# Passes 2 and 3 of a graph kernel: the type sums of all six dense blocks on VectorE

## The reference

```python
x = layernorm(x + wx * segment_sum(w**2 * wx[src], dst))            # layer 0
x = layernorm(x + out @ W2 + b2)    # layer 1: sum of x[src] and edge attributes over dst
h = relu(conv(x)); x = layernorm(x + conv(h))                       # layer 2: two weighted sums
for _ in range(3):                                                  # layer 3
    msg = t[etypes, src]            # t[k] = h @ W_et[k].T + b_et[k], k = 0..3
    a = segment_sum(msg, dst); h = gru_cell(a, h)
```

## Time and profile before

| | us |
|---|---|
| median of three runs | 13733.29 |
| profiled execution, span from first to last instruction | 15388.9 |
| VectorE busy | 6792.6 |
| TensorE matmul busy | 9965.8 |
| GpSimd busy | 9707.6 |

### The profile page before, as it was taken

How to read it: one execution, slowest core, us unless ns; L and a number is a source line. 1 busy time by engine, 2 the same in 40 slices (tenths; PEclk the granted TensorE clock), 3 DMA queues, 4 the chain that set the end, 5 groups by cost and what they waited for, 6 DMA issues and landing times. The chain is left out here.

```text
span 15388.9 us, 172841 instructions
## 1 busy us (share of the span) xinstructions
PE 9965.8 (65%) x37130; PEld 6375.4 (41%) x37131; DVE 6792.6 (44%) x20397; ACT 1404.0 (9%) x4108; POOL 9707.6 (63%) x8863
## 2 busy tenths in 40 slices
PE   6777774444466666555545555588876888677775
PEld 4444444334335444334333333344443444334443
DVE  3333333333367775666656666333332333222223
ACT  1111111111100000000000000100000000000001
POOL 3888887777746666566655555366665666566662
PEclk7555556667787787667767677799997999889887
DMA  8888887777687775677747666477775777467773
GB/s 276 198 198 195 198 180 146 163 162 128 101 223 196 192 193 137 173 192 194 191 125 185 180 180 177 147 210 215 212 195 140 214 212 209 136 183 193 192 191 90
DMA packets 4070001, 2778.79 MB, mean 181 GB/s; under 512 B 430093, under 2 KB 3820298, under 8 KB 4069630
## 3 DMA queue, kind: packets, MB, share of 16 engines
q1 hardware_dynamic: 3529604, 2147.73, 50.7%
q0 software_dynamic: 508368, 612.97, 21.0%
q10 hardware_dynamic: 31722, 15.04, 0.3%
HBM read 2025.54 MB, written 778.19 MB: 182 GB/s over the span
## 5 line engine op out<-in xcount | busy, mean ns | idle before, releaser
L1012 POOL DMA_INDIRECT ring<-t_types,stage x3408 | 3273.1, 960 | 2164.6 <-issue 1349.2
L1012 POOL DMA_INDIRECT ring<-t_x,stage x2272 | 2213.4, 974 | 1450.6 <-issue 887.6
L1544 PE MATMUL bank<-work 128*128 128x512 f32 x5216 | 2624.0, 647 | 596.7 <-DMA work<-t_types 241.1
L1566 PE MATMUL bank<-ring 128*128 128x128 f32 x13632 | 2260.0, 320 | 974.6 <-DMA ring<-t_types,stage 236.2
L1566 PEld LDWEIGHTS bank<-ring 128*128 128x128 f32 x13632 | 2102.0, 229 | 1754.9 <-issue 1461.1
L2032 DVE TENSOR_REDUCE work<-work 128x512 f32<-128x2048 f32 x524 | 1911.5, 3648 | 1012.6 <-DMA work<-t_pairs 931.0
L968 POOL DMA_INDIRECT t_sums<-ring,stage x1136 | 1766.0, 1555 | 432.1 <-issue 262.4
L2007 DVE TENSOR_TENSOR acc<-acc,bank 128x128 f32 x1704 | 480.9, 282 | 3267.0 <-remote 2074.2
L1544 PEld LDWEIGHTS bank<-work 128*128 128x128 f32 x5216 | 1035.5, 210 | 1734.9 <-issue 1378.9
L1012 POOL DMA_INDIRECT ring<-t_h,stage x1136 | 1080.1, 951 | 782.3 <-ACT stage L1214 407.5
L1549 PE MATMUL bank<-work 128*128 128x512 f32 x1048 | 733.6, 788 | 454.8 <-issue 273.3
(11 more groups left out here) (298 smaller groups left out, 11271.9 us busy)
## 6 DMA issues: line engine op xcount, KB each, us to landing
work<-t_pairs SPq DMA_DIRECT2D x2352, 512.0 KB
t_pairs<-acc SPq DMA_DIRECT2D x272, 740.0 KB
t_pairs<-acc SPq DMA_DIRECT2D x272, 370.0 KB
t_pairs<-acc SPq DMA_DIRECT2D x74, 1360.0 KB
work<-t_types SPq DMA_DIRECT2D x294, 256.0 KB
t_types<-work SPq DMA_DIRECT2D x144, 512.0 KB
ring<-t_types,stage POOLq DMA_INDIRECT x3408
ring<-t_x,stage POOLq DMA_INDIRECT x2272
```

The source lines that it names most:

```text
L1012: pool.indirect_dma_start(msg[:, u, :], None, table, bass.IndirectOffsetOnAxis(ap=stage[:, u:u + 1], axis=0)).then_inc(slot_dma[u], 16)
L1544: mm = pe.matmul(bank[4 + half][:, :], dense_t[:, tile, k_ * D:(k_ + 1) * D] if ph > 3 else dense_x[:, tile, :], dense_b[:, half, k_ * 4:( ...
L1566: mm = pe.matmul(bank[q][:, 0:P], msg[:, u, :], hot[:, u, :], start=k_ == 0, stop=k_ == K - 1)
```

## The change

All six units of a pair are summed by type on VectorE in passes 2 and 3, as in pass 1; TensorE then has one matmul of the program in place of four for c = 5; and SyncE waits for `types_summed` before every block of passes 1 to 3.

```diff
-WHOLE = NH * TILES - 1
...
-                wait(sp, types_summed if ph == 1 or ph < 4 and c != (WHOLE + NH) % (NH * TILES) else dense_done, unit - 1 if not isinstance(p, int) or unit > 1 else 0)
+                wait(sp, types_summed if ph < 4 else dense_done, unit - 1 if not isinstance(p, int) or unit > 1 else 0)
...
-                    if ph > 3 or ph > 1 and c == WHOLE:
+                    if ph > 3:
                         pe.wait_ge(dense_in[half], p * (TILES * 32) + ((ph - 1) * ST * 32 + tile * 32 + 32))
                         for k_ in range(KT):
-                            mm = pe.matmul(bank[4 + half][:, :], dense_t[:, tile, k_ * D:(k_ + 1) * D] if ph > 3 else dense_x[:, tile, :],
+                            mm = pe.matmul(bank[4 + half][:, :], dense_t[:, tile, k_ * D:(k_ + 1) * D],
...
                 def type_sums(p, c):
 
                     half, tile = c % NH, c // NH
-                    if ph > 1 and c == WHOLE:
-                        v.wait_ge(types_summed, p * (NH * TILES) + ((ph - 1) * UNITS + c))
-                        v.sem_inc(types_summed, 1)
-                        return
                     v.wait_ge(dense_in[half], p * (TILES * 32) + ((ph - 1) * ST * 32 + tile * 32 + 32))
```

## The result

The changed kernel takes 13691.16 us (median of 11 runs) against 13729.97 of the kernel before (11 runs beside them): ratio 0.9972, 95% interval 0.9964 to 0.998, that is -39 us. Faster was right; the forecast was -81.

The account below looks back on a forecast made before the run. Pass 3 was taken as bound by a loop of unit 5's matmuls, late signal, unit 1's load and VectorE's sums. Pass 3's -115 and pass 2's -16 made -131, x 0.892 -117; midway to -45, -81 gave 13652, range 13545 to 13765.

Parts of the forecast that it names:

- Pass 3 is the one with something to gain, pass 2 nearly nothing: Profile time: pass 3 falls from 51.6 to 48.0 us a pair, pass 2 by only 0.5 from 47.1.
- Added sum at 0: VectorE, passes 2 and 3: 64 added sums of 3.65 us fit into idle time, cost 0, bounds 0 to +234.
- TensorE's shorter work at -1.5: Unit 5, eight matmuls become two: -3.15 us a pair, net -1.5 with the wait for VectorE's sum.
- SyncE's moved wait: Unit 1's load no longer waits for TensorE; VectorE's block wait falls under 4 us a pair in both passes.
- A rule weighed: GpSimd's gathers: VectorE's added reductions don't hold them up, mean stays 950 ns; a two-port instruction would cost +234 us.
- The sum in profile time, -131: Passes 2 and 3: -115 for pass 3 and -16 for pass 2, times 0.892 gives -117.
- Translation: From profile to timed run: truth between -45 and -117 us, middle taken, -81, that is 13652.
- The bound without late signals: Pass 3's loop without late signals, 41.4 us against 40.0 for gathers: only -45 us to be had, pass 2 nothing.
- Hidden: Rival: without the profiler gathers already bound every pass, the removed wait was covered; 13733 within 27, chance 0.23.
- Both passes fall to 45: Rival: late block bursts delay gathers and signals, so passes 2 and 3 reach 45.0 us a pair; -248, 13485, chance 0.11.
- VectorE the pacer: Rival: VectorE's work and waits fill the pair; pass 3 breaks even, pass 2 pays, +80, 13815, chance 0.16.

Follow-up runs that it names:

- e1: The change in pass 3 alone, unit 5 staying with TensorE in pass 2: 13677.39 us, ratio 0.9976 to the kernel before.
- e2: The change in pass 2 alone, unit 5 staying with TensorE in pass 3: 13716.44 us, ratio 1.0001 to the kernel before.
- e4: Changed kernel with TensorE's product of unit 5 made four times in passes 2 and 3: 13696.69 us, ratio 0.9971 to the kernel before.
- e9: Changed kernel with ScalarE's square root one slot later in passes 1 and 3, on the slow chip: 15247.6 us, ratio 0.99 to the kernel before.
- e5: Changed kernel with two more VectorE reductions of unit 5's block in passes 2 and 3, slow chip: 15313.09 us, ratio 0.9942 to the kernel before.
- e8: Kernel before with ScalarE's square root of pass 3 one slot later, on the slow chip: 15301.38 us, ratio 0.9936 to the kernel before.
- e6b: Kernel before with the fourth gather of every slot left out in passes 2 and 3: 13428.67 us beside 13734.52, run once.
- e5r: Changed kernel with two more VectorE reductions of unit 5's block in passes 2 and 3, fast chip: 13766.65 us, ratio 1.0025 to the kernel before.
- b1: Kernel before, with only a lower bound asserted on two numbers the engines load, profiled again: 13717.99 us, ratio 1.0.

## Why the prediction was right in sign and wrong in size

- *Pass 3 is the one with something to gain, pass 2 nearly nothing.* Right, shown by e1 and e2. The reason was half right: the late block was it, but it reached GpSimd through ScalarE's queue at the root, which the prediction didn't name; it named one-hots, and 0.8 us of wait for them was no carrier. The root's wait stood in the trace of the kernel before (8400 to 8800: total us, times, longest), as large as VectorE's wait for blocks:

```profile
ACT std L1258 <- DVE mv L2168: 121.8, 8, 17.7
```

- *Added sum at 0.* Right: VectorE's work is 36.5 us a pair (37.8 foreseen), below 40, and the block wait took it in. TensorE's wait for one-hots in pass 3 rose from 0.1 to 1.4 us a pair, with no effect on the pair.
- *TensorE's shorter work at -1.5.* Nothing of it reached the time: e4 puts the work back and keeps the gain. The wait for unit 5's sum (1.7 at most foreseen) is not among TensorE's waits of pass 3.
- *SyncE's moved wait.* Right: block waits fell to 0.55 us a pair (under 4 foreseen).
- *A rule weighed.* The answer held: gathers stayed at 947 to 949 ns beside six sums.
- *The sum in profile time, -131.* It had -115 for pass 3 and -16 for pass 2. The change alone was never run where the kernel is slow, but two kernels that hold it were. The first line is e9's stretch in pass 3, the second e5's (columns as in the earlier trace rows):

```profile
8400.00:8800.00 400.00, 213.24 (x817) 150.30 (x817) 306.93 (x538) 24.79 (x92) 256.42 (x270) 0.68 0.73 194
8400.00:8800.00 400.00, 220.46 (x779) 151.58 (x778) 339.35 (x551) 22.77 (x89) 250.41 (x264) 0.61 0.72 192
```

A pair takes 47.4 us in e9 and 48.5 in e5, where 48.0 was forecast, from 51.6. From the first gather of pass 3 to its last are 1814.6 us before, 1710.8 in e8, 1674.6 in e9 and 1723.5 in e5. Pass 3's -115 was thus about right for the kind of execution that it was read on. Pass 2's -16 was not to be seen: 272 gathers in 400 us before, 273 in e9, 272 in e5, and e2's +1 on a fast chip.

- *Translation.* This is the step that failed. It left open whether the late signals of the first profile were the profiler's, and put the value in the middle between -45 (none of them in the timed runs) and -117 (all). The timed runs had none: 41.2 us a pair and -39 in all were measured, so pass 3's term of -115 in the profile was worth -38. The bound without late signals, a loop of 41.4 against 40.0, -45, would have been the forecast. That the 41.4 met the measured 41.2 is partly luck, since e6b bounds the loop at 37.2.
- *Rivals.* "Hidden" had the right world (pass 2 at 40.0 us a pair is bound by its gathers, and pass 4 at 40.3 is near that) and missed the 1.2 us of pass 3. "Both passes fall to 45" fell. "VectorE the pacer" did not come about, but e5r shows it 2 us away.

## What to carry to other kernels

Before a gain is summed in profile time, check that the profile's span is the time of the runs; where they differ by 12%, find out first which of the two is to be forecast, and profile again if that can be done. Where only the longer profile is at hand, sum from durations of instructions and without the waits that nothing in the trace explains. When an engine is full (GpSimd here), only what leaves it without work counts: follow its own waits back, and look at what stands ahead of its supplier's instruction in that supplier's in-order queue. One misplaced wait (the square root ahead of an index write) can be cured by making its producer earlier or by changing the order; here the second gave -30 us of the change's -36, with no work added to any engine.

## What the runs showed of the hardware

The same program took 15396.44 us in one batch, on one chip, and 13715 to 13735 in the others, three of which are on record with other chips. That it is the chip, and not a state it was in at the time, one batch can't show. It is not the profiler: in that batch e8's profiled execution took 15298.48 us and the median of its runs is 15301.38. In its profile the waits without a releaser in the trace stand as in the first one (8400 to 8800: total us, times, longest):

```profile
SPq L652 <- remote: 104.8, 8, 13.7
ACT stage L1214 <- remote: 167.9, 12, 15.4
```

Before, has 101.1 and 120.9. In b1, on a fast chip, pass 3 has no such wait: SyncE's load follows TensorE's last matmul by 0.03 us, against 11.4 in the pair of the earlier trace rows. Single instructions of pass 3 last as long in both: gathers 951 and 954 ns, sums 3655 and 3642, and the median matmul of unit 5 is 593 in both. What makes the signals late stays open.
